# Delta net layer: scores, one convolution and the norms of the next head placed ahead of the first growth product, and one scale written ahead of the masked decays

## The reference, cut to what matters

```python
def _L1_attn_ref(hidden_states, W_qkv, W_z, W_a, W_b, conv_w, A_log, dt_bias, norm_w, W_out):
    B, S, HID = (2, 256, 256)
    HV, HK, DK, DV = (32, 16, 128, 128)
    ...
    xp = jnp.pad(qkv, ((0, 0), (KS - 1, 0), (0, 0)))
    conv = sum((xp[:, k:k + Sn, :] * conv_w[:, k] for k in range(KS)))
    mixed = jax.nn.silu(conv)
    ...
    q = _l2norm(q) * DK ** (-0.5)
    k = _l2norm(k)
    g = -jnp.exp(A_log) * jax.nn.softplus(a + dt_bias)
    beta = jax.nn.sigmoid(b)
    def step(state, inp):
        qt, kt, vt, gt, bt = inp
        state = state * jnp.exp(gt)[..., None, None]
        kv = jnp.einsum('bhk,bhkv->bhv', kt, state)
        delta = (vt - kv) * bt[..., None]
        state = state + jnp.einsum('bhk,bhv->bhkv', kt, delta)
        out = jnp.einsum('bhk,bhkv->bhv', qt, state)
        return (state, out)
    ...
    o = o * jax.lax.rsqrt(var + EPS) * norm_w
    o = o * jax.nn.silu(z.reshape(Bn, Sn, HV, DV))
    return o.reshape(Bn, Sn, VAL_DIM) @ W_out.T
```

## Time and profile before

| | us |
|---|---|
| time, median of 3 runs | 1653.85 (1651.97 to 1654.3) |
| profiled execution, its own time | 1650.12 |
| its span in the trace | 1648.1 |
| PE busy / DVE busy | 1540.5 / 1103.1 |
| ACT busy / POOL busy | 595.3 / 602.7 |
| granted TensorE clock, mean | 0.978 of full |

### The profile page before, as it was taken

One profiled execution on the slowest core, in us unless ns is written; L12 is line 12 of the kernel. 1 busy time (PEld: TensorE's weight loads), 2 busy tenths in 40 slices (PEclk: granted clock), 3 DMA queues, 4 the chain that ended last, 5 costly groups with the idle time before them and its releaser, 6 DMA issues. The chain is left out here.

```text
span 1648.1 us, 34046 instructions
## 1 busy us (share of the span) xinstructions
PE 1540.5 (93%) x14224; PEld 1080.6 (66%) x14224; DVE 1103.1 (67%) x1726; ACT 595.3 (36%) x1037; POOL 602.7 (37%) x937
## 2 busy tenths in 40 slices
PE   7999679999997779999999999999999987999999
PEld 3444357877984457677777777777777774555556
DVE  4666496588567677777778777787777734544443
ACT  2322144345334333444444444344444521111110
POOL 1200054244224565554654546555465421000000
PEclk9989889999999899999999999999999998999999
DMA  7533300010000221212212122121221113200000
GB/s 217 158 88 99 77 1 2 14 39 2 1 1 7 58 52 35 54 34 56 48 45 44 34 56 47 45 44 34 56 50 50 24 27 126 86 1 0 13 1 13
DMA packets 150536, 75.76 MB, mean 46 GB/s; under 512 B 128304, under 2 KB 131632, under 8 KB 148592
## 3 DMA queue, kind: packets, MB, share of 16 engines
q1 hardware_dynamic: 150384, 73.60, 17.6%
HBM read 55.73 MB, written 17.83 MB: 45 GB/s over the span
## 5 line engine op out<-in xcount | busy, mean ns | idle before, releaser
L1890 DVE SCALAR_TENSOR_TENSOR W<-PS,wc,W 128x504 f32<-128x504 f32 x375 | 274.8, 733 | 86.6 <-ACT W L1570 77.7
L2230 PE MATMUL PS<-HT,wgu 128*128 128x512 f32 x320 | 143.5, 592 | 0.0
L1570 ACT ACTIVATE W<-PS,wc 128x512 f32<-128x512 f32 x125 | 85.7, 686 | 158.0 <-PE PS L1265 107.2
L1288 PE MATMUL PS<-wz,HT 128*128 128x256 f32 x512 | 124.9, 392 | 5.6 <-DVE z L1906 4.6
L1265 PE MATMUL PS<-HT,wv 128*128 128x512 f32 x252 | 124.4, 616 | 4.3 <-DVE W L1890 4.3
L1437 PE MATMUL PS<-wo,ogT 128*128 128x256 f32 x512 | 118.7, 391 | 7.7 <-DVE dl L1954 5.0
L1265 PE MATMUL PS<-HT,wkq 128*128 128x512 f32 x248 | 119.4, 605 | 0.9 <-DVE W L1890 0.9
L2364 DVE SCALAR_TENSOR_TENSOR act<-th,PS 128x512 f32<-128x512 f32 x48 | 33.0, 687 | 128.1 <-ACT th L2290 128.1
L1288 PEld LDWEIGHTS PS<-wz,HT 128*128 128x128 f32 x512 | 94.6, 192 | 32.0 <-DVE z L1906 16.5
L1437 PEld LDWEIGHTS PS<-wo,ogT 128*128 128x128 f32 x512 | 98.1, 194 | 24.0 <-DVE dl L1954 5.3
L1790 POOL TENSOR_TENSOR rr<-nm,con 128x8 f32<-128x8 f32 x16 | 26.5, 1658 | 233.6 <-DVE nm L1919 233.6
(11 more groups left out here) (284 smaller groups left out, 3145.0 us busy)
## 6 DMA issues: line engine op xcount, KB each, us to landing
a_rows<-AT SPq DMA_DIRECT2D x16, 512.0 KB, 2.6
wk<-in_l0x_k SPq DMA_DIRECT2D x16, 384.0 KB, 3.5
wgu<-in_moe_gu SPq DMA_DIRECT2D x5, 1024.0 KB, 14.8
queries_scratch<-tts SPq DMA_DIRECT2D x32, 128.0 KB, 2.7
wkq<-in_gdn_w SPq DMA_DIRECT2D x16, 256.0 KB, 2.8
wv<-in_gdn_w SPq DMA_DIRECT2D x16, 256.0 KB, 2.8
wz<-in_gdn_w SPq DMA_DIRECT2D x16, 256.0 KB, 3.3
wo<-in_gdn_w SPq DMA_DIRECT2D x16, 256.0 KB, 3.0
```

What stands on the lines that cost most here:

```text
L1288: mm = pe.matmul(PS[:, zbank(j, m), w * 256:(w + 1) * 256], HT[:, k, n * P:(n + 1) * P], wz[:, k * 2 * DK:(k + 1) * 2 * DK], start=(k == 0 ...
L1570: a.activation(acc[:, flows(h, q), :], PS[:, qbank(h, q), :], ACT.Copy, scale=wc[:, h % 2, 4 * c + 3:4 * c + 4]).then_inc(s["tap"], 1)
L1890: v.scalar_tensor_tensor(a0, p0, wc[:, h % 2, 4 * c + 2 - k:4 * c + 3 - k], a0, ALU.mult, ALU.add).then_inc(s["conv"], 1)
L2230: mm = pe.matmul(PS[:, 2 * (i % 2) + w, :], pack[:, k, w, :], HT[:, k, f * N:(f + 1) * N], start=(k == 0), stop=(k == DC - 1))
```

## The change

Four engines' lists are edited; no instruction is added or removed.

- PE, steady heads: `scores(h)` stands ahead of `grow(j, 4)` instead of behind it.
- DVE, steady heads: `conv(h, 4)` and `norms(h)` stand ahead of `update(j, 4)` instead of behind it.
- POOL, every head: sk is written ahead of the two Et instructions and the second power instead of behind them. The counts of the semaphore rr change accordingly: the second square waits for 6 instead of 5.
- ACT, every head: `swap_scale` waits for rr at 5 of the head instead of 6.

```diff
@@ tensor, step(j)
                     cross(j, 4)
                     if beside:
                         project(h, 4)
+                        scores(h)
                     grow(j, 4)
                     if beside:
-                        scores(h)
                         project(h, 5)
                     turn_T(j, 0)
                     turn_T(j, 1)
@@ scalar, swap_scale(h)
-                    a.wait_ge(s["rr"], h * 7 + 6)
+                    a.wait_ge(s["rr"], h * 7 + 5)
@@ gpsimd, factors(h)
                         g.tensor_tensor(Ed[:, hv, :, :], E[:, hv, :, :], each(dd[:, hv, :], S), ALU.mult).then_inc(s["ed"], 1)
+                    g.tensor_tensor(sk[:, par, :], nm[:, kh], rr[:, par, kh], ALU.mult).then_inc(s["rr"], 1)
                     for hv in range(2):
                         g.wait_ge(s["ed"], h * 2 + hv + 1)
                         if h > 0:
                             g.wait_ge(s["pd"], h * 2)
                         g.tensor_tensor(Et[:, hv, :, :], Ed[:, hv, :, :], over(C("upper"), TILES), ALU.mult).then_inc(s["et"], 1)
                     g.tensor_tensor(rr[:, par, qh], nm[:, qh], C("mhalf")[:, qh], ALU.pow).then_inc(s["rr"], 1)
-                    g.tensor_tensor(sk[:, par, :], nm[:, kh], rr[:, par, kh], ALU.mult).then_inc(s["rr"], 1)
-                    g.wait_ge(s["rr"], h * 7 + 5)
+                    g.wait_ge(s["rr"], h * 7 + 6)
@@ vector, step(j)
                         silu(h, 3)
+                        conv(h, 4)
+                        norms(h)
                     update(j, 4)
                     if beside:
-                        conv(h, 4)
-                        norms(h)
                         silu(h, 4)
```

## The result

The changed kernel takes 1678.69 us (median of 3 runs, 1676.48 to 1679.05) against 1653.85 before: ratio 1.015, 95% interval 1.0131 to 1.0168. It is slower by 24.8 us.

The account below looks back on a forecast made before the run. PE, busy 93% of the span, was taken to bound the kernel. Terms 19.4 + 0.8 + 2.4 + 1.7 = 24.3 us on the median of 1653.85 gave 1678 us, range 1665 to 1692.

Parts of the forecast that it names:

- The hole: PE idle before the scores, waiting for the fourth quarter's `silu`: 1.46 us per clean steady head, 19.4 us in all.
- L1836: POOL's output scaling runs into a head's first `silu`: about eight of fourteen heads 0.3 us worse each, 2.4 us.
- Update and turning of T: DVE's update behind the norms ends before PE's `turn_T`, which stands behind `project(h, 5)`: cover 0.8 us, cost nothing.
- The fifth `silu`: On DVE, falls into POOL's first decay and ends 0.35 us late; 0.24 is covered, 0.1 is not.
- sk: Written earlier on POOL, PE gains 0.31 us at the second gate projection; with DVE's lateness net +0.06 a head, 0.8 us.
- Clock: PE at 1.2 GHz behind holes: one stretch costing 1.7 us taken; ends none and six (10 us).

Follow-up runs that it names:

- fill that cost nothing: Changed kernel with one 128x512 and one 128x256 matmul, results overwritten, on PE between project(h, 4) and scores(h): 1674.57 us, ratio 1.0129.

## Why the prediction was right, step by step

- **The hole.** Forecast 1.46 us a clean head, 0.3 in the first, 1.5 in late ones. A clean head got 1.47 longer, and the first waited 0.27, with DVE yB as the releaser as named. That it is a lack of cover and not the scores' place is shown by the fifth projection in the hole (1664) and by fill that cost nothing. Over the steady heads 24.3 us of waits for the scores' input stand in place of 3.5 for Xs: 20.8 more, against 19.4 taken here and 2.4 for L1836.
- **Update and turning of T.** Forecast free, with 0.8 us of cover. Right: L1351 starts 1.92 behind `project(h, 5)` with no wait.
- **The fifth `silu`.** Forecast to meet the first decay and to end 0.35 late. It took 1.08, 0.39 more. That the sixth `silu` would also end later, behind Et, was not foreseen; it hangs on the same chain. The second growth product then started 2.05 behind its projection instead of 1.91, close to the 0.1 of the forecast.
- **sk.** Forecast a gain eaten by that lateness, 0.06 a head net. The net is small as forecast, the reason is not the one given: without the early sk (1679.22) its wait in front of L1623 is gone as well, since the norms end earlier. Taken alone the early sk gains about 3 us.
- **L1836.** Forecast 2.4 us, from a `silu` 0.3 nearer to it. The trace has the fourth quarter late by 0.5 to 1.5 us in six heads, not all of them the late ones of before; summed over the heads that is about 1.4 us more than before, less than taken.
- **Clock.** The term that was mis-sized. One stretch was taken (1.7), with six as the end; the profiled run has five. In these five heads the growth product starts 4.21 to 4.47 us behind the scores instead of 2.83, so each stretch costs 1.4 to 1.6: about 7.6 in all.

The median moved by 24.8 against a forecast of 24.3, but the profiled pair by 28.6. Part of the closeness is therefore luck: the clock term was too small by about 6, L1836's too large by 1, and the two profiled runs differ by more than the medians do. What stays open is why the low clock follows some holes of 2 us and not others: one of 1.96 here had it, one of 2.36 with the two orders alone and one of 2.46 with the norms behind the update had not, and with the fifth projection in the hole two came behind a wait of only 0.93 in front of L1351. The kernel with PE's order alone had more idle time in each head and no low clock at all; no run here separates what differs.

## What to carry to other kernels

Before an instruction is moved ahead on the engine that bounds the stage, look at when its input ends against when that engine would now reach it; the work it jumps over may be the cover of that input. If the chain to the input starts from the same engine, as here, the hole comes back in every turn of the loop; here almost nothing behind it gave the time back. Test the parts of a change apart: here one line of it was a gain and the rest hid it.

## What the runs showed of the hardware

A `silu` on VectorE, both inputs in SBUF, that starts inside a GpSimd instruction on SBUF (the decays L1801, the scaling L1836) ends about 0.54 us behind the end of that instruction. In the steady heads of the changed kernel such a `silu` took 0.72 to 2.16 us instead of 0.68. Inside the power L1790 of the kernel before (834.78, 1.64 us) it took 0.69, so not every GpSimd instruction holds it up. It works the other way too: with the norms behind the update the `silu` starts 0.16 us ahead of that power, which then takes 2.02 us instead of 1.64 in every steady head. Halving the GpSimd instruction brought the longest from 2.16 to 1.43.

In a single-core kernel whose PE is busy 96% of a stage, stretches at 1.2 GHz stood behind five holes of 1.96 to 2.88 us, each costing about 1.5 us; other holes of that size had none. With matmuls without a use in the hole, 1.3 us a head, the steady heads of the profiled execution had no such stretch, and clean heads were no longer for it.
